# An attention and mixture-of-experts layer: expert lists built by one-hot matmuls, shared slices placed at the last experts, the last weight casts issued behind the first shared loads

## The chip, the cores and the metric

The program runs on all 8 cores of one Trainium2 chip. Each core takes 1024 of the 8192 tokens, and no core waits for another. The time of a run is the time of its slowest core in microseconds (us). Engines: PE does matmuls, DVE, ACT and POOL elementwise work and copies, POOL and SP issue most DMAs, and 16 DMA engines per core move the data.

## The reference, cut to what matters

```python
x = _layernorm(x + attn(x, Wq, Wk, Wv, Wo))          # causal, 16 heads of 128
# the feed-forward part, on flat = x (8192 tokens, 2048 wide), D_FF = 1408
h = relu(einsum('td,ndf->ntf', flat, shared_w1) + shared_b1[:, None, :])   # 2 shared experts
out = flat + einsum('ntf,nfd->td', h, shared_w2) + shared_b2.sum(0)
scores = sigmoid(flat @ centroids.T) + bias           # 16 routed experts
vals, idx = top_k(scores, 4)
gating = scatter(vals, idx); gating = gating / clip(gating.sum(-1), 1e-08)
for w1, b1, w2, b2, g in routed:                      # 16 of them
    rout += (relu(flat @ w1 + b1) @ w2 + b2) * g[:, None]
x = _layernorm(x + out + rout)
```

## The kernel before, in words

**Stages.** A core computes K and V of its sequence and attention for its 1024 rows, then the output projection `Wo` with the first norm in tiles of 128 tokens, and the gate scores. All weights come in f32. A load issued by POOL casts to bf16 on the way (`L688`, DMA `ar<-w1x`, `ar<-w2x`, one unit is 128 rows of 2048, 0.5 MB in bf16). `precast` (L237 to L244) also has POOL cast weights from DRAM to a bf16 copy in DRAM, `wpre`: 18 groups of 6 while attention runs (after 126 units there remain 36), and the rest at L545, behind the four loads of `Wo`. Units with a copy are loaded without a cast by SP (`L679`). `PRE_EXPERTS` (L43) says which experts have one: 0, 2, 4, 6, 8, 10, 12. Experts 1, 3, 5, 7, 9, 11, 13, 14, 15 are cast as they are loaded.

**The weights' ring.** Nine slots of SBUF hold units (`pump`, L691). When PE releases a slot, the next unit in order of first use is issued to it. A unit that is half used keeps its slot.

**Lists.** A token goes to four experts. A core takes per expert up to 320 rows, and a flag chooses at run time between this sparse program and one that computes all. Ranks, selection and positions are DVE operations on tiles of 128 x 128 and 128 x 2048 (L850 to L893). DVE makes destinations, then POOL writes token numbers into a DRAM list with 32 indirect scatters (L952, tensor `list_scr`) and reads it back (L961); PE transposes it (L974) and DVE makes the gather and scatter indices. Those 32 scatters run while PE does group 0 and group 1.

**Shared slices.** The two shared experts' 22 slices are cut into groups of 4, 4, 2, 2, 2, 2, 2 and 4 (`GROUPS`, L39). `dense_group` (L737) is a generator of matmul steps: `L752` is the first layer (64 steps for two slices), `L774` the second (64 steps), whose results DVE adds into the token tiles `x_tm` (`L787`). `spend(n)` takes n steps. Groups 0 and 1 are spent around the lists, groups 2 to 6 inside the experts: `FILL_AT` (L41) gives an expert's steps, in 31 portions (`tick`).

**An expert** (L1083): per slice of 128 of the hidden width, 16 matmuls `L1100` and an ACT copy; then in two halves the second layer, `L1127` and `L1133`, whose output DVE (`L1152`) and ACT (`L1154`) copy out and POOL scatters into `y_scr` (L1167). POOL gathers the next expert's rows (L1002), PE turns them (`L1017`), DVE copies them (`L1026`). From expert 13 on `combine_load` (L1056) has SP read back 1 MB blocks of `y_scr` and `combine_add` has DVE add them (`L1071`): 8 blocks per expert, the first three experts' worth inside experts 13, 14, 15, through one buffer, and 8 more in the last shared group. SP and DVE take their work in the order of the program.

## Time and profile before

| | |
|---|---|
| runs, us | 2705.9, 2714.79, 2895.99; median 2714.79 |
| the profiled execution, its own time | 2707.15 |
| span of its slowest core (core 2) | 2705.6 |
| spans of the eight cores | 2652.8 to 2705.6 |
| mean granted TensorE clock | 0.923 to 0.928 |
| busy on core 2: PE, DVE, ACT, POOL | 2249.0, 831.9, 544.7, 411.4 |
| DMA queue 0 (POOL's issues), queue 1 (SP's) | 304.39 MB, 139.90 MB |

The profiled execution lies within 0.3% of the median. Times in the trace count from the span's start: attention to 866, `Wo` and the first norm to 1094, lists and shared groups 0 and 1 to 1289, experts 0 to 15 to 2596, the last shared group and norm to the end. PE's busy time is the sum over matmuls, DMA share the mean over 16 engines; a saturated stretch reads 1.00 to 1.05.

### The profile page before, as it was taken

What the parts mean: (1) busy time and instruction counts of PE and PEld (TensorE: products, weight loads), DVE (VectorE), ACT (ScalarE), POOL (GpSimd) and SP (SyncE); (2) the same over time, 40 slices, a digit from 0 to 9 for tenths busy, and PEclk for the clock granted to TensorE, in tenths of its full rate; (3) what the DMA queues carried; (4) which work ended last, traced back from release to release, by engine and by line L of the source; (5) the groups of instructions that cost most, each with busy time, mean ns of one, the idle gap of its engine ahead of it and who ended that gap; (6) DMA issues with size and microseconds to landing.
All of it is one profiled execution on the core that took longest, in us unless ns stands there. A gap on an engine that the chain in (4) does not pass through costs nothing.

```text
span 2705.6 us, 35359 instructions; the slowest of 8 cores (2652.8 to 2705.6 us)
## 1 busy us (share of the span) xinstructions
PE 2249.0 (83%) x13390; PEld 1192.1 (44%) x13593; DVE 831.9 (31%) x1269; ACT 544.7 (20%) x817; POOL 411.4 (15%) x619
## 2 busy tenths in 40 slices
PE   5879999989888589458979999999999999576456
PEld 3546646646556244123434444454444444233121
DVE  0234434434444334143201041412213041222146
ACT  0033433334343422101111101011111111011003
POOL 1011011111110000140021212121121212111100
PEclk9889999999999689678999999999999999787788
DMA  9499999999996999912599998989898999999973
GB/s 161 65 120 121 121 122 122 121 122 120 120 118 104 160 165 139 142 46 83 170 164 264 171 242 197 205 228 176 248 180 254 175 247 196 208 222 215 202 243 125
DMA packets 114655, 446.65 MB, mean 165 GB/s; under 512 B 16244, under 2 KB 16916, under 8 KB 104752
## 3 DMA queue, kind: packets, MB, share of 16 engines
q0 software_dynamic: 81360, 304.39, 72.6%
q1 hardware_dynamic: 33120, 139.90, 15.6%
q8 instruction: 114, 1.87, 0.3%
q14 instruction: 61, 0.50, 0.1%
HBM read 647.80 MB, written 139.50 MB: 291 GB/s over the span
## 4 chain that ended last, share of the span: by engine, by line
DMA 50%; PE 36%; DVE 5%; issue 4%; another core or an unknown queue 3%; ACT 1%; POOL 1%; DVEq 0%; ACTq 0%; POOLq 0%; SPq 0%
DMA wpre<-w2x 14%; DMA wpre<-w1x 12%; DMA ar<-y_scr 10%; PE PP L1127 9%; PE PP L1100 7%; PE PP L774 5%; DMA ar<-w1x 5%; DMA ar<-w2x 5%; PE PP L1133 3%; PE PP L323 2%; PE PP L342 2%; PE PP L752 2%; DMA ar<-wqkv 2%; PE PP L1017 2%
## 5 line engine op out<-in xcount | busy, mean ns | idle before, releaser
L1100 PE MATMUL PP<-ar 128*128 128x320 bf16 x2816 | 411.4, 305 | 53.1 <-DMA ar<-w1x 48.3
L1127 PE MATMUL PP<-ar 128*128 128x512 bf16 x1363 | 373.3, 396 | 24.8 <-DMA ar<-w2x 17.4
L1100 PEld LDWEIGHTS PP<-ar 128*128 128x128 bf16 x2816 | 276.6, 100 | 188.5 <-issue 71.8
L323 PE MATMUL PP<-ar 128*128 128x512 bf16 x992 | 238.6, 383 | 30.3 <-DMA ar<-wqkv 29.1
L774 PE MATMUL PP<-ar 128*128 128x512 bf16 x680 | 191.5, 407 | 81.2 <-DVE ar L787 48.7
L478 ACT COPY ar<-PP 128x1024 bf16<-128x1024 bf16 (+1 forms) x192 | 153.4, 799 | 474.0 <-PE PP L467 474.0
L342 PE MATMUL PP<-ar 128*128 128x256 bf16 x2048 | 241.5, 273 | 0.0
L1026 DVE COPY ar<-PP 128x960 bf16<-128x960 bf16 x96 | 55.4, 598 | 587.5 <-PE PP L1017 587.5
L437 DVE TENSOR_REDUCE st_sb<-PP 128x1 f32<-128x256 f32 (+7 forms) x128 | 173.7, 1357 | 169.7 <-PE PP L431 150.5
L787 DVE SCALAR_TENSOR_TENSOR ar<-PP,ar 128x512 f32<-128x512 f32 x256 | 167.2, 687 | 167.9 <-PE PP L774 124.6
L342 PEld LDWEIGHTS PP<-ar 128*128 128x128 bf16 x2048 | 197.7, 98 | 30.3 <-issue 0.2
L1127 PEld LDWEIGHTS PP<-ar 128*128 128x128 bf16 x1408 | 121.8, 100 | 190.1 <-issue 85.0
L752 PE MATMUL PP<-ar 128*128 128x512 bf16 x669 | 162.9, 384 | 43.4 <-DMA ar<-w1x 40.1
L1107 ACT ACTIVATE ar<-PP,b_sb 128x320 bf16<-128x320 f32 x176 | 92.8, 527 | 419.3 <-PE PP L1100 404.7
L1154 ACT COPY ar<-PP 128x512 f32<-128x512 f32 x64 | 34.4, 589 | 696.0 <-PE PP L1133 696.0
L307 PE MATMUL PP<-ar 128*128 128x512 bf16 (+1 forms) x576 | 131.4, 371 | 40.2 <-DMA ar<-xT 29.5
L1071 DVE SCALAR_TENSOR_TENSOR ar<-ar,gk_sb 128x2048 f32<-128x2048 f32 x32 | 75.2, 2351 | 269.9 <-DMA ar<-y_scr 269.7
L447 ACT ACTIVATE ar<-PP,st_sb 128x256 bf16<-128x256 f32 (+7 forms) x128 | 157.0, 1226 | 0.5 <-DVE st_sb L437 0.5
L323 PEld LDWEIGHTS PP<-ar 128*128 128x128 bf16 x1024 | 97.2, 99 | 132.8 <-issue 39.2
L1133 PE MATMUL PP<-ar 128*64 128x512 bf16 x704 | 147.7, 416 | 0.3
L1167 POOL DMA_INDIRECT y_scr<-ar,sidx_sb x96 | 96.0, 1000 | 305.4 <-DVE ar L1152 284.4
L1017 PE MATMUL PP<-cb_sb,ar 128*128 128x128 bf16 (+1 forms) x768 | 97.6, 221 | 47.7 <-DVE ar L1026 45.9
(110 smaller groups left out, 1784.5 us busy)
## 6 DMA issues: line engine op xcount, KB each, us to landing
ar<-wpre SPq DMA_DIRECT2D x162, 512.0 KB
ar<-w1x POOLq DMA_DIRECT2D x117, 512.0 KB
ar<-w2x POOLq DMA_DIRECT2D x117, 512.0 KB
wpre<-w1x POOLq DMA_DIRECT2D x81, 512.0 KB, 24.7
wpre<-w2x POOLq DMA_DIRECT2D x81, 512.0 KB, 24.7
ar<-y_scr SPq DMA_DIRECT2D x32, 1024.0 KB
ar<-wqkv POOLq DMA_DIRECT2D x24, 1024.0 KB
ar<-xT POOLq DMA_DIRECT2D x8, 1024.0 KB
```

Source lines behind the costliest of these rows:

```text
L323: (lambda e, dc=dc: e.matmul(ps, w_at["k"][:, dc * 256 + jl * 128: dc * 256 + (jl + 1) * 128], x_bf[:, c * 8192 + dc * 512: c * 8192 + (dc ...
L342: (lambda e, dc=dc, tl=tl, sub=sub: e.matmul(ps[:, sub * 256:(sub + 1) * 256], x_bf[:, c * 8192 + dc * 512 + tl * 128: c * 8192 + dc * 512 ...
L437: sb.do("vector", lambda e: e.reduce_max(negmx_sp[up], PP[:, 0:kc], axis=AX.X, negate=True), "dv", 1)
L447: lambda e: e.activation(p_sb[up][:, 0:kc], PP[:, 0:kc], AF.Exp, bias=negmx_sp[up], scale=1.0, accum_out=lsum_sp[up]),
L478: lambda e: e.copy(dst, tb[:, 0:nbl * 128].rearrange("p (kb n) -> p kb n", n=128)), "ac", 1)
L752: m = sb.mm((lambda e, dc=dc, w=w, bank=bank, nt=nt: e.matmul(psum_bank(bank), w[:, dc * 128:(dc + 1) * 128], xhat[:, dc * 1024 + nt * 512 ...
L774: m = sb.mm((lambda e, j=j, w=w, bank=bank, ti=ti, dn=dn, last=last: e.matmul(psum_bank(bank), Hs[j][:, ti * 128:(ti + 1) * 128], w[:, dn ...
L787: give_bank(bank, sb.vec((lambda e, xs=xs, bank=bank, sc=sc: e.scalar_tensor_tensor(xs, psum_bank(bank), sc, xs, ALU.mult, ALU.add))))
L1017: m = sb.mm((lambda e, n=n, dc=dc, t=t, rows=rows: e.transpose(tb[:, n * CAP + t * 128: n * CAP + t * 128 + rows], xg[t][0:rows, dc * 128: ...
L1100: m = sb.mm((lambda e, dc=dc, w=w, bank=bank: e.matmul(psum_bank(bank)[:, 0:CAP], w[:, dc * 128:(dc + 1) * 128], xgT[:, dc * CAP:(dc + 1) ...
L1127: sb.mm((lambda e, fc=fc, w=w, po=po, t=t, dn=dn: e.matmul(psum_bank(2 * t + dn), Hr(fc)[:, t * 128:(t + 1) * 128], w[:, po * 1024 + dn * ...
L1133: m = sb.mm((lambda e, fc=fc, w=w, po=po, dn=dn, end=end: e.matmul(PP[dn * 64:(dn + 1) * 64, 4 * 512:5 * 512], Hr(fc)[:, 256:CAP], w[:, po ...
```

## The change

It has five parts.

1. The lists. Each (expert, token tile) pair gets one DVE operation that compares the row of slot numbers with the token's position, 128 x 320 in bf16, and one matmul of that one-hot block against two columns per expert (token number within the tile; eight times the choice plus the tile's number plus one). 128 such pairs accumulate in one PSUM bank over twelve buffers. The result is copied, transposed and decoded into the same indices. The DRAM list, its fill, 32 scatters, 4 loads and the destination arithmetic go.
2. The stored gates and their transposes move behind that loop; 96 steps of group 0 stand inside it, 6 per expert.
3. `FILL_AT`: 64 at experts 3, 7, 11 and 12 and 128 at 13, 14 and 15, where it was 128 at 3, 5, 7, 9 and 11.
4. `PRE_EXPERTS`: 14 in the place of 12.
5. Behind `Wo` only 16 casts are issued; the last 20 come behind the first eight shared loads. The sparse program stands ahead of the dense one.

DVE also waits for the last write of a piece of `x_tm` before it adds to it again (`x_mark`).

```diff
-FILL_AT = {0: 72, 3: 128, 5: 128, 7: 128, 9: 128, 11: 128}
+FILL_AT = {0: 72, 3: 64, 7: 64, 11: 64, 12: 64, 13: 128, 14: 128, 15: 128}
-PRE_EXPERTS = (0, 2, 4, 6, 8, 10, 12)
+PRE_EXPERTS = (0, 2, 4, 6, 8, 10, 14)
...
-        precast(len(PRE_UNITS))
+        precast(PRE_WO)
...
         set_plan(plans["common"] if plans else [])
+        precast(len(PRE_UNITS))
         state["gen"] = dense_group(GROUPS[0], nt_outer=True)
...
+        sb.vchain(lambda e: e.tensor_scalar(pos, sel, -FAR, FAR - SHIFT, ALU.mult, ALU.add))
+        pos_dv = sb.vchain(lambda e: e.tensor_tensor(pos, pos, pbank[:, 0:128], ALU.add))
+        sb.vchain(lambda e: e.memset(vz, 0.0))
...
+        sb.wait("tensor", *vz_dv)
+        sb.wait("tensor", *pos_dv)
+        sb.wait_all("vector", u_stored)
+        for n in range(16 * 8):
+            ei, ti = divmod(n, 8)
+            buf = n % len(one_hot)
+            if oh_free[buf] is not None:
+                sb.wait("vector", *oh_free[buf])
+            m = sb.vec(lambda e, buf=buf, c=ti * 16 + ei: e.tensor_scalar(
+                one_hot[buf], iota_sb, pos[:, c:c + 1], None, ALU.is_equal))
+            if ti == 0:
+                spend(6)
+            sb.wait("tensor", *m)
+            oh_free[buf] = sb.mm((lambda e, buf=buf, n=n, c=ti * 512 + ei * 32: e.matmul(
+                pbank[0:32, 0:CAP], vz[:, c:c + 32], one_hot[buf],
+                start=(n == 0), stop=(n == 127), skip_group_check=True)), True)
...
-        for c in range(8 * KR):
-            sb.dma("gpsimd", (lambda e, c=c: e.indirect_dma_start(
-                out=list_scr, out_offset=IOA(ap=dest_sb[:, c:c + 1], axis=0),
...
-            if b % 2:
-                spend(6)
+            spend(3)
...
-            if j == 12:
+            if j == NR - 1:
                 spend(100000)
...
+                with e.If(flag < 1):
+                    play(e, sparse_ops[eng])
                 with e.If(flag > 0):
                     play(e, dense_ops[eng])
-                with e.If(flag < 1):
-                    play(e, sparse_ops[eng])
```

POOL's issues from the loads of `Wo` on. Before (`L242` is a cast into `wpre`, `L688` a casting load into the ring):

```order
L242 DMA wpre<-w1x 128x2048 x3
L242 DMA wpre<-w2x 128x2048 x11
L242 DMA wpre<-w1x 128x2048 x11
L242 DMA wpre<-w2x 128x2048 x11
L688 DMA ar<-w1x 128x2048 x4
L688 DMA ar<-w2x 128x2048 x4
```

and now (one line down or up: `L246` is the cast, `L687` the load, `L1028` the gather of expert 0):

```order
L246 DMA wpre<-w1x 128x2048 x3
L246 DMA wpre<-w2x 128x2048 x11
L246 DMA wpre<-w1x 128x2048 x2
L687 DMA ar<-w1x 128x2048 x4
L687 DMA ar<-w2x 128x2048 x4
L246 DMA wpre<-w1x 128x2048 x9
L246 DMA wpre<-w2x 128x2048 x11
L1254 TENSOR_LOAD flag_sb
L1255 COMPARE_AND_BRANCH
L1028 DMA ar<-u_scr,gidx_sb 128x2048 x2
L1028 DMA ar<-u_scr,gidx_sb 64x2048
```

The eight shared loads now stand behind 16 casts instead of 36, and the other 20 casts stand ahead of the flag and the gathers.

DVE in the list stage. Before, behind the last of the destination arithmetic:

```order
L890 TENSOR_REDUCE ar<-ar 128x8
L891 SCALAR_TENSOR_TENSOR ar<-ar 128x128
L892 TENSOR_REDUCE gk_sb<-ar 128x8
L893 CAST dest_sb<-ar 128x32
L787 SCALAR_TENSOR_TENSOR ar<-PP,ar 128x512 x5
L903 MEMSET ar 18x1024
L905 CAST ar<-PP 16x512
L906 CAST ar<-PP 16x512
L787 SCALAR_TENSOR_TENSOR ar<-PP,ar 128x512 x27
```

and now (`L903` is the one-hot comparison, `L789` the addition into `x_tm` that was `L787`); the pattern of the last rows goes on over 16 experts:

```order
L883 TENSOR_TENSOR ar<-ar,PP 128x128
L886 MEMSET ar 128x4096
L889 CAST ar<-cf_sb 128x8x16
L890 SCALAR_TENSOR_TENSOR ar<-ar,cf_sb 128x8x16
L903 TENSOR_SCALAR ar<-cb_sb,ar 128x320
L789 SCALAR_TENSOR_TENSOR ar<-PP,ar 128x512
L903 TENSOR_SCALAR ar<-cb_sb,ar 128x320 x8
L789 SCALAR_TENSOR_TENSOR ar<-PP,ar 128x512
L903 TENSOR_SCALAR ar<-cb_sb,ar 128x320 x8
L789 SCALAR_TENSOR_TENSOR ar<-PP,ar 128x512 x2
L903 TENSOR_SCALAR ar<-cb_sb,ar 128x320 x8
```

Each eight comparisons are followed by one or two additions that wait for PE.

PE at expert 5. Before, its first layer (`L1100`) with shared steps (`L752`) between:

```order
L1127 MATMUL PP<-ar 128x512 x4
L1133 MATMUL PP<-ar 64x512 x2
L1100 MATMUL PP<-ar 128x320 x16
L752 MATMUL PP<-ar 128x512 x4
L1100 MATMUL PP<-ar 128x320 x16
L752 MATMUL PP<-ar 128x512 x4
L1100 MATMUL PP<-ar 128x320 x16
L752 MATMUL PP<-ar 128x512 x4
```

and now, with `L1127` as the first layer, `L1154`, `L1160` as the second, `L1146` as the reset of a bank:

```order
L1154 MATMUL PP<-ar 128x512 x4
L1160 MATMUL PP<-ar 64x512 x2
L1154 MATMUL PP<-ar 128x512 x4
L1160 MATMUL PP<-ar 64x512 x2
L1127 MATMUL PP<-ar 128x320 x176
L1146 MATMUL PP<-ar,cb_sb 128x512
L1154 MATMUL PP<-ar 128x512 x4
L1160 MATMUL PP<-ar 64x512 x2
L1154 MATMUL PP<-ar 128x512 x4
```

The shared steps are gone from expert 5; rows such as those of before now stand at experts 12 to 15, where before there was one row of 176.

## Rows read from the trace of the kernel before

**Rows 1.** Page of the slowest core: mean busy tenths of its 16 DMA engines, 40 slices.
```profile
DMA  9499999999996999912599998989898999999973
```

**Rows 2.** Windows: span; PE, PEld, DVE, ACT, POOL busy (count); PEclk, DMA share, GB/s.
```profile
1579.00:1655.00 76.00, 74.61 (x435) 36.69 (x438) 23.68 (x38) 9.03 (x17) 13.69 (x15) 0.98 0.89 251
...
1655.00:1730.00 75.00, 72.20 (x402) 35.33 (x408) 11.16 (x18) 9.43 (x17) 18.45 (x29) 1.00 1.01 176
...
1760.00:1765.00 5.00, 5.00 (x39) 3.62 (x37) 0.00 (x0) 1.05 (x2) 2.36 (x3) 1.00 0.99 319
...
2187.00:2273.00 86.00, 85.26 (x492) 40.70 (x497) 23.91 (x39) 9.07 (x18) 19.52 (x23) 1.00 0.88 239
```

**Rows 3.** Timeline around the first shared weights: start, duration (us), engine, line [idle before].
```profile
996.04 0.52 POOL L242 DMA_DIRECT2D wpre<-w1x  x1 [7.12 <-DMA wpre<-w2x]
...
1111.98 0.52 POOL L242 DMA_DIRECT2D wpre<-w2x  x1 [5.83 <-DMA wpre<-w2x]
...
1112.54 2.15 POOL L688 DMA_DIRECT2D ar<-w1x  x4
...
1134.23 11.39 PE L752 MATMUL PP<-ar 128*128 128x512 bf16 x38 [40.15 <-DMA ar<-w1x]
```

**Rows 4.** Timeline of the list stage, DVE, POOL and PE.
```profile
1162.89 0.23 DVE L857 CAST ar<-ar 128x128 bf16<-128x128 f32 x1
...
1164.99 2.29 DVE L879 TENSOR_TENSOR ar<-ar,cb_sb 128x2048 bf16<-128x2048 f32 x1
...
1181.35 0.91 DVE L903 MEMSET ar<- 18x1024 bf16 x1 [0.34 <-DVE ar L787]
...
1218.35 0.97 POOL L952 DMA_INDIRECT list_scr<-cf_sb,dest_sb  x1 [0.30 <-issue]
...
1238.92 27.57 PE L752 MATMUL PP<-ar 128*128 128x512 bf16 x124 [1.77 <-issue]
```

**Rows 5.** DVE groups by form: count, busy us, mean ns of one, idle before.
```profile
L453 DVE TENSOR_SCALAR ar<-ar,st_sb 128x512 bf16<-128x512 bf16 x16 | 5.6, 353 | 1.7
...
L453 DVE TENSOR_SCALAR ar<-ar,st_sb 128x256 bf16<-128x256 bf16 x16 | 4.6, 286 | 1.7
...
L787 DVE SCALAR_TENSOR_TENSOR ar<-PP,ar 128x512 f32<-128x512 f32 x256 | 167.2, 687 | 167.9 <-PE PP L774 124.6
```

**Rows 6.** Timeline in attention: a POOL issue beside a DVE operation.
```profile
374.59 0.88 POOL L242 DMA_DIRECT2D wpre<-w2x  x1 [4.62 <-DMA wpre<-w2x]
...
374.73 0.62 DVE L453 TENSOR_SCALAR ar<-ar,st_sb 128x1536 bf16<-128x1536 bf16 x1
```

**Rows 7.** Timeline, ACT and DVE copies that close experts 0, 1, 2, 4, 11, 12, 15.
```profile
1368.65 1.07 ACT L1154 COPY ar<-PP 128x512 f32<-128x512 f32 x2 [25.93 <-PE PP L1133]
...
1451.51 1.07 ACT L1154 COPY ar<-PP 128x512 f32<-128x512 f32 x2 [20.68 <-PE PP L1133]
...
1516.88 1.07 ACT L1154 COPY ar<-PP 128x512 f32<-128x512 f32 x2 [21.41 <-PE PP L1133]
...
1667.95 1.07 ACT L1154 COPY ar<-PP 128x512 f32<-128x512 f32 x2 [19.52 <-PE PP L1133]
...
2213.96 1.07 ACT L1154 COPY ar<-PP 128x512 f32<-128x512 f32 x2 [25.75 <-PE PP L1133]
...
2272.95 1.07 ACT L1154 COPY ar<-PP 128x512 f32<-128x512 f32 x2 [17.12 <-PE PP L1133]
...
2595.59 1.88 DVE L1152 COPY ar<-PP 128x512 f32<-128x512 f32 x3
```

**Rows 8.** Timeline, first casting loads of experts 1 and 3, and one in a saturated stretch.
```profile
1489.78 0.58 POOL L688 DMA_DIRECT2D ar<-w1x  x1 [32.50 <-PE PP L1133]
...
1860.35 0.53 POOL L688 DMA_DIRECT2D ar<-w2x  x1 [2.86 <-DMA ar<-w2x]
```

**Rows 9.** Timeline, one DVE add of a combined row block in expert 13.
```profile
2319.01 2.35 DVE L1071 SCALAR_TENSOR_TENSOR ar<-ar,gk_sb 128x2048 f32<-128x2048 f32 x1 [11.58 <-DMA ar<-y_scr]
```

More of the change, by code:

```diff
@@ L231, in build_nc @@
     g_sb = carve(77056, 256, F32)
+    lrow = carve(77312, 2 * LCAP, F32)
+    vz = carve(23552, 4096)
+    one_hot = [carve(98304 + CAP * i, CAP) for i in range(12)]
     def emit(plans):
@@ L252, in emit @@
         ]
-        sb.vec(lambda e: e.memset(fill_sb[:, :], EMPTY))
-        sb.wait("sync", "dv")
-        fill_mark = sb.dma("sync", lambda e: e.dma_start(out=list_scr.rearrange("(p j) c -> p (j c)", p=128),
-                                                         in_=fill_sb[:, :]))
         def load_w(kind, g):
@@ L732, in emit @@
         hs_free = [None]
+        x_mark = {}
         def w2_kind(ge):
@@ L786, in dense_group @@
                     xs = x_tm[ti][:, dn * 512:(dn + 1) * 512]
-                    give_bank(bank, sb.vec((lambda e, xs=xs, bank=bank, sc=sc: e.scalar_tensor_tensor(
-                        xs, psum_bank(bank), sc, xs, ALU.mult, ALU.add))))
+                    if (ti, dn) in x_mark:
+                        sb.wait("vector", *x_mark[ti, dn])
+                    x_mark[ti, dn] = sb.vec((lambda e, xs=xs, bank=bank, sc=sc: e.scalar_tensor_tensor(
+                        xs, psum_bank(bank), sc, xs, ALU.mult, ALU.add)))
+                    give_bank(bank, x_mark[ti, dn])
                 if after_tile is not None:
@@ L915, in emit @@
         saved = ({k: (dict(v) if k in ("at", "load") else v and list(v)) for k, v in ring.items()},
-                 {b: list(v) for b, v in rb.items()}, list(hs_free))
+                 {b: list(v) for b, v in rb.items()}, list(hs_free), dict(x_mark))
         sb = root.branch_off()
@@ L936, in emit @@
         sb = root.branch_off()
-        ring, rb, hs_free = saved
+        ring, rb, hs_free, x_mark = saved
         saved = None
@@ L947, in limit @@
             return limit_regs[value]
-        sb.wait("gpsimd", *dest_dv)
-        sb.wait("gpsimd", *fill_mark)
-        for c in range(8 * KR):
-            sb.dma("gpsimd", (lambda e, c=c: e.indirect_dma_start(
-                out=list_scr, out_offset=IOA(ap=dest_sb[:, c:c + 1], axis=0),
-                in_=rid_sb[:, c:c + 1], in_offset=None,
-                bounds_check=limit(e, NR * LCAP - 1), oob_is_err=False)), pool="gs")
-        sb.wait_all("gpsimd", sb.dma_total_marks("gs"))
-        list_rows = list_scr.rearrange("(e s) c -> e (s c)", e=16)
-        lrow = tmp[9]
-        list_marks = []
-        for r0, s0, n, c0 in ((0, 0, 128, 0), (16, 128, 128, 0), (32, 256, 64, 0), (32, 256, 64, 64)):
-            list_marks.append(sb.dma("gpsimd", (lambda e, r0=r0, s0=s0, n=n, c0=c0: e.dma_start(
-                out=lrow[r0:r0 + 16, c0:c0 + n], in_=list_rows[:, s0:s0 + n])), pool="gs"))
         def chain_groups():
@@ L1072, in combine_add @@
             ybufs.append([buf, m, None])
+            for dn in range(4):
+                x_mark[ti, dn] = m
         pend = []
```

101 lines of the change are left out of this document (57 added, 44 removed).

## The prediction

> **What bounds the kernel now.** I read the page's slices first. DMA is at nine tenths or more in most slices from attention to the end, with two holes: the list stage (2 in slice 18) and the very end [rows 1]. So from expert 1 on one has to ask of every change both what it does to PE and what it does to DMA. Second, two windows that follow each other and make up one period of the pattern of a plain and a casting expert: in the second, PE is busy 72 of 75 us and DMA reads 1.01, in the first PE is busy 74.6 of 76 us and DMA 0.89, the clock nearly full in both [rows 2]. The middle is bound by PE and DMA almost equally. Third, the timeline where the first shared weights arrive: PE starts its first shared matmul at 1134.2 after 40.15 us idle, so it was done with `Wo` and the gate scores at 1094.1. It waited for a load that POOL issued only at 1112.5, after its last cast [rows 3]. Fourth, the ends of experts: 0 ends at 1368.7, 1 at 1451.5, 2 at 1516.9, 4 at 1668.0, 11 at 2214.0, 12 at 2273.0, 15 at 2595.6 [rows 7]. Three facts are in these. Experts 3 and 4, with 128 shared steps, took 151.1 us; experts 1 and 2, with none, took 148.2; experts 13, 14, 15 took 322.6, or 107.5 each, with no shared steps at all but 8 blocks of `y_scr` each.
>
> **Prices of transfers.** Two casting loads in a saturated stretch stand 3.4 us apart (0.53 and the 2.86 before it), and several such in a row average 3.3; I take 3.28 [rows 8]. A plain unit is 0.52 MB at the 319 GB/s of a stretch that has only such loads, 1.64 us [rows 2]. An expert's scatter and gather are some 3.4 MB at that rate, 11 us (an estimate). A pair then needs 26 x 3.28 + 22 x 1.64 + 22 = 143 us; the two windows give 76 x 0.89 + 75 x 1.01 = 143 as well. In experts 13 to 15, (107.5 - 72 - 11) / 8 leaves 3.1 us for each block. The chain of reads alone costs the same: 11.58 us of waiting and 2.35 of adding, 13.9 x 8 = 111 [rows 9]. So there both DMA and the one buffer bind.
>
> **Part 5, the casts behind the first loads.** The 16th cast behind `Wo` went out at 996.0 and the last, the 36th, at 1112.0: 5.8 us each [rows 3]. Now POOL is through with 16 at 996, and the loads wait only for their slots, the first of which the last `Wo` tile frees some ten us before 1094 (three of its four sets of 16 matmuls at 0.22 us come after). The DMA queue is then empty of casts, and units land every 3.3 us while PE takes 16 x 0.216 = 3.5 us for each half of a slice. PE goes on at 1094: 40 us saved. After the wait PE ran 38 matmuls in 11.39 us, 0.300 each, where 124 full-speed ones took 27.57 with their gaps, 0.22 [rows 3, 4]: 3 us more. Together -43. The other 20 casts go behind 8 loads (27 us from 1083): 1110 + 16 x 5.8 = 1203 for the last issue. They stand ahead of the flag and of expert 0's gather, which is due at about 1235 (below). They fit into the hole of the list stage, with 32 us to spare; without that cover each us is paid in full at expert 0.
>
> **Parts 1 and 2, the lists.** Before, from the selection (`L857`, 1163.1) to group 1 (`L752`, 1238.9) passed 75.8 us, though the 32 scatters ended only at 1219.3 [rows 4]. PE was never held by the list itself, so its removal frees nothing directly; what goes is PE's slow crawl beside the scatters. New: two operations of 2.3 us (`L879` and its sum, moved up), seven small ones (2 us), and a memset of 4096 columns, four times the 0.91 us for 1024 [rows 4]: 10 us, with PE idle. Then the loop. A comparison is a `TENSOR_SCALAR` in bf16 from SBUF: 286 ns at 256 columns, 353 at 512, hence 303 at 320 [rows 5]. Per expert: 8 x 0.303 = 2.4, one and a half additions at 0.687 = 1.0, and about 0.6 in which DVE waits for the four shared matmuls ahead of the addition. That is 4.0, and 64 us for sixteen. PE's 8 small matmuls run behind the comparisons. Bounds: below, 128 x 0.303 and half the additions hidden, 47; above, every comparison at the 0.687 of `L787`, 88. Then thirteen small operations (5.5), the last 32 shared steps with their additions (5.5), the gate transposes (2). In all 87 against 75.8: +11, with bounds of -6 and +35. Five more small DVE operations ahead of the gather cost +2. The additional DVE waits (`x_mark`) are for work of a whole group earlier and cost nothing, since the same 32 additions stand between.
>
> The Trainium skill (VectorE: DVE Perf Modes, "The perf-mode tier table") says that a scalar operation on bf16 in SBUF runs at four elements per cycle. The slope of rows 5, 67 ns for 256 columns, agrees; what it does not shrink is the fixed 0.22 us, which is three quarters of each comparison.
>
> **Parts 3 and 4, experts.** Fill is 64 less at experts 3, 7, 11 and 128 less at 5, 9. A casting expert is not bound by PE once its fill is gone. A pair with 64 steps loads 24 casts, 137 us; with none, 130. I keep the idle 8 us per pair (76 x 0.11, where slots are full and the next casts not yet due [rows 2]): 145 and 138 against 151. Four pairs: -(6 + 13) x 2 = -38. Bounds: experts 1 and 2 show 148 without fill, which would give -10; PE alone (128 x 0.216 = 27.6 us) would give -83. Experts 11 to 15 get what the others lose: 12 casts, 39 us. Expert 12 took 59 us because its loads were plain; with 24 casts it needs about 90. Expert 14, now plain, gives the same back. Against that, the idle DMA time in expert 12 (86 x 0.12 = 10 us [rows 2]) goes, and about 9 more (an estimate) where casts waited for slots behind the block reads. Tail: +39 - 19 = +20. The fill's PE work, 27.6 us an expert, finds room in 107.5 us, since experts without it are done by PE in 59 (expert 12). Its additions, 32 x 0.69, lie on DVE between block adds, in the 11.6 us in which DVE waits anyway. Experts together: -18.
>
> The sum: -43 + 11 + 2 - 18 = -48. From the execution's own 2707.15 that is 2659; the median of the runs is 0.3% above it, and I say 2660.
>
> **Rivals.**
>
> *DMA overlaps better* (0.24). The idle 8 us per pair disappear too, since PE now waits for slots less, and the list loop comes near its lower bound. For: the clock and both engines have no other limit there. Against: experts 1 and 2. 2707 - 43 - 6 + 2 - 55 = 2605.
>
> *Moved, not saved* (0.12). The experts are one long DMA queue and gain nothing: 2707 - 43 + 13 = 2677. For it speak experts 1 and 2, against it that their casts began only 15 us before the expert, where expert 3's began 27 us before [rows 7, 8].
>
> *POOL is held up by the comparisons* (0.08). A cast's issue that lay beside one comparison-like operation took 0.88 us instead of 0.52 [rows 6]. If POOL can't issue while DVE goes through 128 of them, the 16 late casts slip by up to 64 us, to 1267, the gather lands 20 us behind that instead of at about 1242, and expert 0 starts 45 us late: 2704. One row with 0.36 us more speaks rather for a cost of a few us in the slack. The Trainium skill (SBUF — State Buffer, "A bandwidth-pool intuition that's wrong (but worth ruling out)") describes that: POOL can't write descriptors until the vector operation releases a port that they share.
>
> *The tail pays in full* (0.14), the one that ends slower. In experts 13 to 15 DVE waits in program order for a block read; PE's fill needs DVE for every four steps and has three banks. If PE can't get ahead, fill and waiting add instead of overlapping: 3 x 27.6 = 83, and 34 at expert 12, tail +117. With -30 from the front and -39 in the middle that is 2755. It decides from a tail of +69 on. For: PE's work is small in 107.5 us there, and yet nothing goes faster. Against: DVE is idle in each wait, the additions stand ahead of the block add in its order, and four steps of an expert with fill fill the 13.9 us.
>
> **How the numbers follow.** Forecast 0.42, own range 2635 to 2685. A measurement of this kernel tells about 2% from no change: 2660. The forecast lies on that line, so I split it 0.20 and 0.22. Faster by over 2%: 0.20 + 0.24 = 0.44. Within: 0.22 + 0.12 + 0.08 and 0.06 of the tail's rival, 0.48. Slower: 0.08. The range goes from just below the better overlap, 2598, to 2715, which leaves out the tail's rival.
>
> **What would show it.** PE's wait of 40 us before the first shared step gone; the last cast issued at about 1203 and ahead of the first gather; comparisons near 0.30 us, the loop near 64; group 1 starting 32 us earlier than now, expert 0 about 30; experts 5 and 6 in 138, 12 in about 90, 13 to 15 in 310 to 330 together. I am wrong if experts 3 to 10 give under 20 or over 60 us, if 13 to 15 take over 360, or if POOL's issues stretch beside the comparisons.

## The result, and the profile after

The changed kernel ran in 2636.41, 2642.31 and 2644.44 us, median 2642.31, against 2714.79 before: a ratio of 0.9744, with a 95% interval of 0.9692 to 0.9797. (Executions in which the cores of one die ran at a lower granted clock are left out of every comparison; the experiment with the comparisons ahead has only two others, and in its profile, where cores 4 to 7 had 0.80 to 0.81, a core of the other die is read.) The profiled execution took 2636.41 us where that of before took 2707.15, so 70.7 less; the forecast had 48 less. Below, the numbers of before stand in the rows ahead of the prediction.

The page of the slowest core (again core 2, span 2634.7 us), granted clock and DMA share in 40 slices:

```profile
PEclk9989999999999779999999999999999998999888
DMA  9499999999998895597499898989898999989973
```

Against [rows 1] the list stage is no longer empty (slices 17 and 18, counted from 0, read 9 and 7 instead of 1 and 2), but slices 15 and 16 ahead of it now read 5 and 5: a new hole.

Timeline where the first shared weights arrive, as in [rows 3]: start, duration, engine, line (`L598` is `Wo`, `L687` a casting load, `L246` a cast into `wpre`, `L1028` the gather):

```profile
1081.21 2.14 POOL L687 DMA_DIRECT2D ar<-w1x  x4 [81.68 <-PE PP L598]
...
1092.09 8.58 PE L752 MATMUL PP<-ar 128*128 128x512 bf16 x39
...
1200.81 0.52 POOL L246 DMA_DIRECT2D wpre<-w2x  x1 [4.15 <-DMA wpre<-w2x]
...
1236.72 1.07 POOL L1028 DMA_INDIRECT ar<-u_scr,gidx_sb  x1 [35.39 <-DVE ar L789]
```

PE goes from the gate scores to the first shared step without a wait. The last cast is issued at 1200.8 (forecast 1203), 36 us ahead of the gather, which is issued at 1236.7 (forecast 1235).

The list stage, as in [rows 4, 5]. First the end of the selection and the loop on DVE and PE (`L861` closes the selection as `L857` did before, `L903` is the comparison, `L908` its matmul, `L789` the addition into `x_tm`), then the group of all 128 comparisons (busy us, mean ns), then the start of group 1:

```profile
1117.94 0.23 DVE L861 CAST ar<-ar 128x128 bf16<-128x128 f32 x1
...
1125.21 3.47 DVE L886 MEMSET ar<- 128x4096 bf16 x1 [0.99 <-DVE ar L883]
...
1147.99 1.78 DVE L903 TENSOR_SCALAR ar<-cb_sb,ar 128x320 bf16<-128x320 bf16 x8
...
1149.94 1.47 PE L774 MATMUL PP<-ar 128*128 128x512 bf16 x6
1150.87 0.69 DVE L789 SCALAR_TENSOR_TENSOR ar<-PP,ar 128x512 f32<-128x512 f32 x1 [1.09 <-PE PP L774]
...
1151.91 1.57 PE L908 MATMUL PP<-ar 128*32 128x320 bf16 x7 [0.27 <-DVE ar L903]
```

```profile
L903 DVE TENSOR_SCALAR ar<-cb_sb,ar 128x320 bf16<-128x320 bf16 x128 | 28.6, 296 | 0.0
```

```profile
1204.90 27.57 PE L752 MATMUL PP<-ar 128*128 128x512 bf16 x127
```

DVE waits 1.09 us for PE's six shared steps, then PE waits 0.27 for DVE's next comparison: the two take turns. The loop runs from 1129.9 to 1190.0.

The copies of ACT that close experts 0, 2, 10, 11 and 12, as in [rows 7] (now `L1181`), and PE's first step of the last shared group:

```profile
1336.31 1.07 ACT L1181 COPY ar<-PP 128x512 f32<-128x512 f32 x2 [24.27 <-PE PP L1160]
...
1480.62 1.07 ACT L1181 COPY ar<-PP 128x512 f32<-128x512 f32 x2 [20.91 <-PE PP L1160]
...
2030.76 1.07 ACT L1181 COPY ar<-PP 128x512 f32<-128x512 f32 x2 [19.52 <-PE PP L1160]
...
2109.45 1.07 ACT L1181 COPY ar<-PP 128x512 f32<-128x512 f32 x2 [0.89 <-PE PP L1160]
...
2196.31 1.07 ACT L1181 COPY ar<-PP 128x512 f32<-128x512 f32 x2 [23.84 <-PE PP L1160]
...
2516.49 27.80 PE L752 MATMUL PP<-ar 128*128 128x512 bf16 x128
```

In the kernel before, expert 10 ended at 2125.3 and PE took the last shared group up at 2579.0, some 17 us before DVE's copy at 2595.6 that [rows 7] have as the end of expert 15:

```profile
2125.32 1.07 ACT L1154 COPY ar<-PP 128x512 f32<-128x512 f32 x2 [20.71 <-PE PP L1133]
...
2578.95 27.80 PE L752 MATMUL PP<-ar 128*128 128x512 bf16 x125
```

Windows, columns as in [rows 2]: the new hole, a pair without shared steps (experts 5 and 6), and expert 13, 14, 15:

```profile
1003.00:1040.00 37.00, 34.14 (x217) 17.58 (x216) 16.84 (x34) 10.19 (x7) 0.00 (x0) 0.95 0.56 138
1040.00:1081.00 41.00, 41.00 (x258) 20.23 (x256) 21.12 (x46) 9.26 (x8) 0.00 (x0) 1.00 0.07 26
...
1620.00:1696.00 76.00, 63.37 (x364) 30.94 (x363) 7.68 (x14) 8.34 (x16) 17.21 (x25) 0.96 1.02 205
1696.00:1755.00 59.00, 59.00 (x360) 29.84 (x359) 7.13 (x13) 7.94 (x15) 12.90 (x16) 1.00 0.86 237
...
2197.00:2311.00 114.00, 92.64 (x483) 42.44 (x482) 42.71 (x51) 10.88 (x20) 19.88 (x28) 0.91 1.00 231
2311.00:2405.00 94.00, 87.58 (x486) 41.84 (x483) 45.18 (x52) 10.41 (x19) 12.57 (x18) 1.00 0.89 252
2405.00:2518.00 113.00, 88.90 (x444) 39.88 (x445) 42.84 (x48) 10.60 (x20) 19.98 (x32) 0.92 1.00 214
```

In the pair without shared steps the casting expert has PE busy 63 of 76 us with DMA full, so only DMA binds there; in the plain expert behind it PE is busy all 59 us and DMA 0.86. In experts 13 and 15 DMA is full and PE has 21 and 24 us to spare; in expert 14, whose loads are plain, DMA reads 0.89 and PE has 6.

Where the 70.9 us between the spans went, stage by stage, each from the rows above and those of before:

| stage | before | after | change | forecast |
|---|---|---|---|---|
| start to the end of the selection | 1163.1 | 1118.2 | -45.0 | -43 |
| selection to group 1 | 75.8 | 86.7 | +10.9 | +11 |
| group 1 to the end of expert 0 | 129.7 | 131.4 | +1.7 | +2 |
| experts 1 and 2 | 148.2 | 144.3 | -3.9 | 0 |
| experts 3 to 10 | 608.4 | 550.1 | -58.3 | -38 |
| expert 11 to PE's last group | 453.6 | 485.7 | +32.1 | +20 |
| from there to the end | 126.7 | 118.2 | -8.5 | 0 |

The column of before is core 2, and for the list stage that matters. From the end of the selection to group 1 the other cores of its die (0 to 3) took 75 to 81 us in the same profile, but cores 4 to 7 only 47 to 50. In the changed kernel all eight take 86 to 88. In the kernel before, while the 32 scatters run, DVE on cores 0 to 3 stands idle for 3 to 11 us before single additions, with no releaser in the profile; on core 2 the four matmuls that an addition needs had ended 2 to 7 us before it began. PE goes on when the addition is done. Core 2 of the kernel before, then core 5, where the same steps run without a break:

```profile
1202.04 0.69 DVE L787 SCALAR_TENSOR_TENSOR ar<-PP,ar 128x512 f32<-128x512 f32 x1 [5.65 <-remote]
1202.88 1.86 PE L774 MATMUL PP<-ar 128*128 128x512 bf16 x4 [5.32 <-issue]
...
1210.48 0.69 DVE L787 SCALAR_TENSOR_TENSOR ar<-PP,ar 128x512 f32<-128x512 f32 x1 [7.75 <-issue]
...
1220.26 0.69 DVE L787 SCALAR_TENSOR_TENSOR ar<-PP,ar 128x512 f32<-128x512 f32 x1 [9.10 <-remote]
```

```profile
1185.03 23.10 PE L774 MATMUL PP<-ar 128*128 128x512 bf16 x105
```

Four such gaps of DVE on core 2 come to 26 us; cores 4 to 7 have none above 2 us. So the slowest core of cores 4 to 7 went only from 2675.6 to 2631.2, 44 us, where the slowest of all went from 2705.6 to 2634.7. In each of the 21 runs of the kernel before that list their cores, the slowest core of one die, always the same die of a chip, was 11 to 39 us above that of the other; in the six of the changed kernel the two lay within 9 us. Only one of the 21 was profiled. That the others lose the time in the same way is likely but not shown, and why one die has the gaps is open.

### The profile page after: what moved, and what is told of

Its sections match the earlier page's. It is cut to its first block, busy times and chain, and to the rows that moved or that the text cites. A ratio compares the mean times of both kernels' runs of the same rounds, so it can differ in the third digit from the quotient of the medians.

```text
span 2634.7 us, 36044 instructions; the slowest of 8 cores (2594.9 to 2634.7 us)
## 1 busy us (share of the span) xinstructions
PE 2296.7 (87%) x13723; PEld 1200.7 (46%) x13723; DVE 865.8 (33%) x1397; ACT 544.2 (21%) x817; POOL 377.8 (14%) x583
## 4 chain that ended last, share of the span: by engine, by line
DMA 49%; PE 38%; DVE 6%; issue 4%; ACT 2%; POOL 1%; DVEq 0%; POOLq 0%; SPq 0%; ACTq 0%
DMA wpre<-w1x 12%; DMA wpre<-w2x 12%; DMA ar<-w2x 8%; PE PP L1154 8%; PE PP L1127 8%; DMA ar<-y_scr 6%; DMA ar<-w1x 5%; PE PP L774 4%; PE PP L598 3%; PE PP L1160 3%; PE PP L752 2%; PE PP L1043 2%; PE PP L322 2%; PE PP L341 2%; DVE ar L1096 1%
## 5 line engine op out<-in xcount | busy, mean ns | idle before, releaser
L1127 PE MATMUL PP<-ar 128*128 128x320 bf16 x2816 | 413.0, 305 | 44.0 <-DMA ar<-w1x 37.4
L1154 PE MATMUL PP<-ar 128*128 128x512 bf16 x1408 | 379.6, 394 | 17.5 <-DMA ar<-w2x 17.4
L1127 PEld LDWEIGHTS PP<-ar 128*128 128x128 bf16 x2816 | 276.4, 99 | 182.6 <-issue 64.2
L322 PE MATMUL PP<-ar 128*128 128x512 bf16 x1024 | 244.4, 382 | 29.4 <-DMA ar<-wqkv 29.3
L774 PE MATMUL PP<-ar 128*128 128x512 bf16 x704 | 208.4, 411 | 68.2 <-DVE ar L789 47.5
L789 DVE SCALAR_TENSOR_TENSOR ar<-PP,ar 128x512 f32<-128x512 f32 x256 | 169.8, 688 | 218.8 <-PE PP L774 203.3
L1154 PEld LDWEIGHTS PP<-ar 128*128 128x128 bf16 x1408 | 124.7, 100 | 189.4 <-issue 76.9
L752 PE MATMUL PP<-ar 128*128 128x512 bf16 x704 | 174.0, 382 | 12.8 <-DVE ar L890 8.8
L1181 ACT COPY ar<-PP 128x512 f32<-128x512 f32 x64 | 34.4, 589 | 633.5 <-PE PP L1160 633.5
L1160 PE MATMUL PP<-ar 128*64 128x512 bf16 x704 | 146.8, 414 | 0.0
L466 PE MATMUL PP<-cb_sb,ar 128*128 128x128 bf16 x1152 | 101.3, 227 | 37.5 <-ACT ar L477 32.5
L687 POOL DMA_DIRECT2D ar<-w1x x117 | 65.1, 561 | 450.7 <-PE PP L1160 247.2
```

Of the source, the lines that this page charges most:

```text
L322: (lambda e, dc=dc: e.matmul(ps, w_at["k"][:, dc * 256 + jl * 128: dc * 256 + (jl + 1) * 128], x_bf[:, c * 8192 + dc * 512: c * 8192 + (dc ...
L752: m = sb.mm((lambda e, dc=dc, w=w, bank=bank, nt=nt: e.matmul(psum_bank(bank), w[:, dc * 128:(dc + 1) * 128], xhat[:, dc * 1024 + nt * 512 ...
L774: m = sb.mm((lambda e, j=j, w=w, bank=bank, ti=ti, dn=dn, last=last: e.matmul(psum_bank(bank), Hs[j][:, ti * 128:(ti + 1) * 128], w[:, dn ...
L789: x_mark[ti, dn] = sb.vec((lambda e, xs=xs, bank=bank, sc=sc: e.scalar_tensor_tensor(xs, psum_bank(bank), sc, xs, ALU.mult, ALU.add)))
L1127: m = sb.mm((lambda e, dc=dc, w=w, bank=bank: e.matmul(psum_bank(bank)[:, 0:CAP], w[:, dc * 128:(dc + 1) * 128], xgT[:, dc * CAP:(dc + 1) ...
L1154: sb.mm((lambda e, fc=fc, w=w, po=po, t=t, dn=dn: e.matmul(psum_bank(2 * t + dn), Hr(fc)[:, t * 128:(t + 1) * 128], w[:, po * 1024 + dn * ...
```

## Experiments

Twelve kernels on three chips, four on each; ratios are to the kernel before on the same chip, with 95% intervals. The kernel before had medians of 2705.2, 2704.2 and 2735.2 on the three. The changed kernel ran in the first comparison (0.9744, chip not noted) and on the second of the three chips. The table below gives, from each profile, what groups of experts took (start of DVE's copy that closes one to the next, to 0.2 us, slowest core unless a core is named), and the time from the end of expert 12 to the end of the program:

| kernel | expert 0 ends | 1, 2 | 3 to 10 | 11, 12 | 13 to 15 | 12 to the end |
|---|---|---|---|---|---|---|
| before (first profile) | 1368.7 | 148.3 | 608.4 | 147.6 | 322.6 | 432.6 |
| changed (first profile) | 1336.3 | 144.4 | 550.1 | 165.5 | 321.9 | 438.3 |
| changed again, core 0 / core 4 | 1335.2 / 1330.5 | 142.4 / 141.9 | 548.2 / 550.0 | 165.7 / 164.3 | 337.2 / 327.9 | 449.4 / 443.6 |
| all casts at `Wo` | 1379.8 | 147.7 | 547.3 | 165.3 | 327.0 | 442.4 |
| only part 5 | 1379.9 | 148.8 | 599.0 | 148.8 | 321.8 | 429.3 |
| old `FILL_AT` and `PRE_EXPERTS` | 1334.5 | 141.9 | 599.5 | 147.6 | 326.5 | 441.9 |
| old `FILL_AT` alone | 1329.4 | 141.3 | 603.7 | 155.0 | 317.4 | 433.0 |
| lists alone | 1393.0 | 150.9 | 607.8 | 147.1 | 324.8 | 433.6 |
| more steps in the tail, core 0 / core 4 | 1324.2 / 1346.8 | 141.8 / 143.9 | 522.6 / 540.9 | 157.1 / 167.0 | 356.3 / 353.3 | 476.0 / 470.4 |
| sixteen more casts | 1383.8 | 144.6 | 551.1 | 155.5 | 322.2 | 439.3 |
| twelve casts in the hole | 1351.0 | 147.0 | 555.8 | 154.3 | 319.4 | 435.7 |
| hole and ahead | 1347.2 | 148.3 | 553.8 | 157.0 | 321.2 | 435.2 |
| the same, even fill | 1346.7 | 147.7 | 569.1 | 154.7 | 323.0 | 441.3 |

Two things in the cores bear on every reading. In each of the neighbouring pairs of cores (0 and 1, 2 and 3, 4 and 5, 6 and 7) one is slower, in the changed kernel by 21 to 41 us, and which of the two it is differs from execution to execution. In the first profile of the changed kernel the slower four (0, 2, 4, 7) took 550 to 555 us for experts 3 to 10, the faster four 525 to 536. The slower four set the time, so only slower cores are compared with slower ones. The other is the difference between the dies of the kernel before: where it matters, runs are set against its faster die too.

### Which part carries the gain

**Part 5 undone.**

```diff
-PRE_WO = 16
+PRE_WO = 162
```

> The changed kernel with all 36 casts behind Wo again (part 5 undone). My theory: PE again waits some 40 us for the first shared weights, nothing later absorbs it, because expert 0 has idle DMA time either way: 40 to 44 us slower than the changed kernel, group 1 starting some 41 us later than at 1205, experts 1 to 15 as they are. Rival (one long DMA queue: the casts cost the same wherever they stand, so an earlier start of the experts is given back there): 0 to 15 us slower.

Measured: ratio 0.9912 (0.9877 to 0.9947), runs from 2681.57 to 2685.68 us; by the ratios 37 to 45 us above the changed kernel. The wait is back:

```profile
1138.91 10.68 PE L752 MATMUL PP<-ar 128*128 128x512 bf16 x39 [39.12 <-DMA ar<-w1x]
```

Expert 0 ends 43.5 us later, experts 3 to 10 take 547.3. Nothing absorbs it, and the rival of one long queue falls.

**Part 5 alone.**

```diff
-        precast(len(PRE_UNITS))
+        precast(16)
...
+        precast(len(PRE_UNITS))
         state["gen"] = dense_group(GROUPS[0], nt_outer=True)
```

> The kernel before with part 5 alone: 16 casts behind Wo, 20 behind the first eight shared loads, lists by 32 indirect scatters as before. My theory: part 5 needs part 1. PE starts the shared steps at 1094 instead of 1134, but the scatters stand behind the last cast on POOL (about 1203), end at about 1244 and the gather is issued at about 1258 instead of 1269; PE runs out of shared steps and waits. About 11 us faster than before, at most 20. Rival (the parts are independent): 40 us faster than before.

Measured: 1.002 (0.9996 to 1.0043), nothing won; I had expected 11 us. The two dies are within 13 us of each other now: on the die that was faster before (slowest core 2673 to 2683 us) the kernel is some 32 us slower (2703 to 2722), on the other it is level. Timeline of PE and POOL (`L242` a cast, `L953` a scatter into the list, `L975` the list's transpose):

```profile
1094.37 8.58 PE L752 MATMUL PP<-ar 128*128 128x512 bf16 x39
...
1277.68 0.31 PE L975 MATMUL PP<-cf_sb,ar 48*128 48x48 f32 x1 [77.86 <-DMA ar<-list_scr]
```

```profile
1214.24 0.52 POOL L242 DMA_DIRECT2D wpre<-w2x  x1 [6.52 <-DMA wpre<-w2x]
1228.53 1.06 POOL L953 DMA_INDIRECT list_scr<-cf_sb,dest_sb  x1 [13.77 <-issue]
...
1267.91 0.97 POOL L953 DMA_INDIRECT list_scr<-cf_sb,dest_sb  x1 [0.27 <-issue]
```

PE starts 40 us earlier and then waits 78 us for the list. The mechanism was the one expected, its size was not: the casts went out at 6 us each until 1214, and another 13.8 us passed before the first scatter, put down to no releaser (8 to 14 us on the eight cores). Expert 0 ends 11 us later than in the first profile of before.

**Parts 1 and 2 alone.** The diff is that of the first experiment together with both old tables.

> The changed kernel with parts 3, 4 and 5 undone: the new lists alone, all casts behind Wo, the old FILL_AT and PRE_EXPERTS. My theory: alone they cost what their stage shows, +10.9 us in the list stage and some 2 ahead of the gather, and save nothing; 8 to 14 us slower than before, the DMA engines idle for some 60 us in the list stage. Rival (they shorten something by themselves, the POOL engine free of 32 scatters): not slower than before.

Measured: one run, 2734.47, against runs of before from 2727.98 to 2741.96 on that chip. No interval: on the slowest core it shows no large gain or loss, and neither the 8 to 14 us nor the rival is settled by it. From the first shared step to group 1 pass 115.0 us in its profile against 104.7 on core 2 of before, so the stage's own loss of 10 is there; cores 4 to 7 of before took 75 to 78. The runs show more: on the chip's faster die the slowest core had 2702 to 2704 us before and has 2722.9 now, 20 us more, on the slower die 2726 to 2740 and 2732.4. With the gaps away the new lists alone cost time.

Read together, by the slowest core: lists alone about nothing, casts alone nothing, both together (the next kernel) 0.9841. On the faster die: 20 us lost, 32 lost, and 13 won (2676 to 2662 us on the first chip). The parts are complements: the lists free POOL, and that gives the late casts a place. But of the 40 us that they give together some 27 are the difference of the dies, which either part alone also removes.

**Parts 3 and 4 undone.**

```diff
-FILL_AT = {0: 72, 3: 64, 7: 64, 11: 64, 12: 64, 13: 128, 14: 128, 15: 128}
-PRE_EXPERTS = (0, 2, 4, 6, 8, 10, 14)
+FILL_AT = {0: 72, 3: 128, 5: 128, 7: 128, 9: 128, 11: 128}
+PRE_EXPERTS = (0, 2, 4, 6, 8, 10, 12)
```

> The changed kernel with the old FILL_AT and the old PRE_EXPERTS (parts 3 and 4 undone). My theory: the stretch from expert 3 to the end is what these two parts decide; it took 1188.7 us before and 1154.1 after, so 35 us slower than the changed kernel (30 to 40), experts 3 to 10 near 608 and experts 13 to 15 near 322. Rival (part of the middle's gain beyond the forecast comes from the new front, through the state in which the ring enters expert 1): 10 to 20 us slower, experts 3 to 10 near 590.

Measured: 0.9841 (0.9810 to 0.9871). The changed kernel has 0.9775 on the second chip and 0.9744 in the first comparison, so 18 to 26 us, less than the 35 expected and near the rival's 10 to 20; but the rival's 590 for the middle did not come. Experts 3 to 10 took 599.5, not 608; the kernel with part 5 alone, whose middle is that of before, took 599.0 too, and in the first profile of before the seven other cores took 596 to 601. So some 8 us of the first comparison's 58 belong to core 2 of that execution and not to the edit. The tail spreads between cores of one execution: for experts 13 to 15, by ACT's copies, the four slower cores of the changed kernel took 318 to 322 us in the first profile and 314 to 335 in the second.

From expert 12 to the end this kernel needs 433 to 442 us on its slower cores and lists alone 434 to 439, against 428 to 434 in before and in part 5 alone, which have the same tables. So some 5 us come with the new program itself. The added waits (`x_mark`) would be a reason; they were not tried alone.

**`FILL_AT` alone undone.**

> The changed kernel with the old FILL_AT alone; expert 12 is still cast as it loads and 14 is plain. My theory: shared steps cost 1 us for 8 in the casting experts of the middle and almost nothing in experts 13 to 15, where DMA and the block reads bind: experts 3 to 11 take 68 us more, 12 some 3 to 6 less, 13 to 15 within 10 us of 321, the end 7 less: 50 us slower (40 to 60). Rival (the shared steps of the tail are paid there too): experts 13 to 15 get up to 83 us faster, and the kernel stays within 10 us of the changed one.

Measured: 0.9833 (0.9803 to 0.9862), level with the kernel before it, so 16 to 24 us above the changed one. Both theories miss: experts 3 to 11 take 62 more where 68 were expected, experts 13 to 15 get only 4.5 faster (10 to 20 against the second chip), not 83; what I had wrong is expert 12, at 67.4 instead of 84, though it casts. A reason, which no run here separates, is that behind a 128-step expert 11, in which PE sets the pace, DMA gets ahead by what nine slots hold. The two experts together take 155.0 against 165.5.

**Still more in the tail.**

```diff
-FILL_AT = {0: 72, 3: 64, 7: 64, 11: 64, 12: 64, 13: 128, 14: 128, 15: 128}
+FILL_AT = {0: 72, 11: 64, 12: 64, 13: 192, 14: 128, 15: 192}
```

> The changed kernel with the 64 shared steps of experts 3 and 7 moved on to 13 and 15 (192 each). My theory: 64 steps in a pair of the middle cost 4 to 10 us (138.7 and 144.2 against 133.6 without), and in experts 13 and 15 PE still has 20 us to spare, so 10 to 15 us faster. Rival (the tail is full: the clock is already 0.91 to 1.00 there and PE is busy 93 of 114 us in expert 13): experts 13 and 15 get up to 14 us longer each and the kernel is 5 to 15 us slower.

Beside it ran the changed kernel once more:

> The changed kernel once more, on the chip on which the next three run, so that they have it beside them. The first profile gave 2636.41 us; 2634 to 2645 is expected, experts 3 to 10 together 550 us within 5, the stretch from expert 13 to 15 within 5 of 322.

Measured: changed again 0.9775 (0.9747 to 0.9803), more steps 0.9831 (0.9777 to 0.9885), runs of 2649 to 2671 against 2643 to 2646. The intervals overlap, but every run is slower, by 22 us in the median: the rival has the direction, and it costs more than its 5 to 15. Core 0 is the faster of its pair in the one profile and the slower in the other, so it can't be compared. Over the four slower cores of each, experts 3 to 10 give back 8 us (552 to 543 in the mean) and 13 to 15, by ACT's copies, take 26 more (325 to 351). The changed kernel once more came as expected in the middle, but 13 to 15 took 337.2 in it, outside its band.

From these runs the price of 64 shared steps follows. In experts 3 to 10: 550.1 with two such portions, 599 to 604 with eight, hence 8 to 9 us each; but the first two cost only about 4 each (the 8 us above). In the tail the first six portions cost 15 to 30 us together (experts 11 to 15: 472.4 without, 487.4 to 502.9 with), 2.5 to 5 each, and the next two about 14 each (490 to 518 for experts 11 to 15 over the slower cores). The table of the changed kernel lies about where the two prices meet.

### What sets the list loop

```diff
+        LEAD = 6
-        for n in range(16 * 8):
+        for step in range(16 * 8 + LEAD):
...
-            sb.wait("tensor", *m)
+            sb.wait("tensor", *oh_done[n])
```

The comparison of step n is issued by DVE before the shared steps and the matmul of step n - 6.

> The changed kernel with the one-hot comparisons running six ahead of their matmuls. My theory: the list loop (60 us, 3.70 an expert) is bound neither by DVE's comparisons (8 x 0.222 = 1.78 an expert) nor by PE, but by the two taking turns: DVE waits 1.09 or 0.83 us per expert for the four shared matmuls, PE 0.3 to 0.7 for the next comparison. With the turns gone DVE binds at 1.78 + 1.03 = 2.8 an expert, 45 us: 12 to 15 us faster, all of it seen at expert 0. Rival (PE's own work, 6 shared steps and 8 small matmuls, is the limit): within 4 us of the changed kernel.

Measured: 0.9715 (0.9686 to 0.9743) against 0.9775 (0.9747 to 0.9803) on the same chip; 2626.84 and 2629.46 us against a median of 2642.85, so 15 us. It is faster than both kernels, if by two runs only. Core 3, DVE (`L906` is the comparison here) and then PE:

```profile
1138.69 1.78 DVE L906 TENSOR_SCALAR ar<-cb_sb,ar 128x320 bf16<-128x320 bf16 x8
1140.39 1.32 DVE L789 SCALAR_TENSOR_TENSOR ar<-PP,ar 128x512 f32<-128x512 f32 x2
1141.62 1.78 DVE L906 TENSOR_SCALAR ar<-cb_sb,ar 128x320 bf16<-128x320 bf16 x8
```

```profile
1185.59 27.57 PE L752 MATMUL PP<-ar 128*128 128x512 bf16 x127
```

From the third expert on no wait is left on DVE; two experts take 5.23 us instead of 7.39, and the comparisons run from 1126.3 to 1170.4. Expert 0 ends at 1321.2 on both slower cores of the die, 9 and 14 us earlier than on those of the changed kernel on that chip, and the gain is still there at the end.

### Where more casts fit

**Sixteen more, in the list stage and expert 0.**

```diff
+    units += [... the first 16 units of expert 12 ...]
...
-        precast(len(PRE_UNITS))
+        precast(len(PRE_UNITS) - len(pre_mark) - EXTRA + EXTRA_EARLY)
...
+                if j == 0 and step % 2 == 0:
+                    precast(1)
```

> The changed kernel with 16 units of expert 12 cast ahead of time as well, 6 of them behind the last casts in the list stage and 10 inside expert 0, where the DMA engines are 0.47 to 0.58 busy. My theory: DMA time that stands idle before expert 1 is worth as much as any; 16 casts are 52 us of it against 51 idle, and expert 12 then loads 16 units plain, 26 us less: 15 to 25 us faster, expert 12 at 62 to 70 instead of 87. Rival (POOL in its order: ten casts at 4.8 us hold up the scatters of expert 0 and the first casting loads of expert 1): expert 1 ends 20 us later and nothing is left of it.

Measured: 0.9879 (0.9857 to 0.9902), 31 us slower than the changed kernel beside it. Neither mechanism: it is not POOL's order that holds the kernel up, but PE's waits for landings. Expert 0 ends some 50 us late; experts 1 and 2 take 144.6, as before. PE waits for the gathered rows and, in expert 0, for plain loads:

```profile
1264.01 0.26 PE L1046 MATMUL PP<-cb_sb,ar 128*128 128x128 bf16 x1 [15.50 <-DMA ar<-u_scr,gidx_sb]
...
1302.94 3.31 PE L1132 MATMUL PP<-ar 128*128 128x320 bf16 x16 [3.18 <-DMA ar<-wpre]
```

DMA issues of the stretch 1260 to 1330 (KB each, median us from issue to landing):

```profile
ar<-wpre SPq DMA_DIRECT2D x11, 512.0 KB, 24.4
wpre<-w1x POOLq DMA_DIRECT2D x5, 512.0 KB, 24.9
```

A plain load that needs 1.64 us of DMA time lands 24 us after its issue beside four casts, and the ring has only nine slots. The Trainium skill (DMA: Bandwidth & Descriptors, "Queues, rings and completion order") says that a DMA engine serves the queues that have work in turn, packet by packet; the two kinds of transfer with equal landing times fit that. The added casts did not spread over the idle time either: DMA reads 1.00 from 1243 to 1264, while the gather lands, 0.12 from there to 1283, and 0.99 from 1283 to 1330, where PE is busy 33 of 47 us. A DMA share of 0.58 in a stretch that PE drains in step is not 0.42 of free time.

**Twelve, into the hole.** 28 casts behind `Wo`, and 12 units of expert 12 more.

```diff
-PRE_WO = 16
+PRE_WO = 28
+    units += [("w1", 14, u) for u in range(FCH)] + [("w2", 14, 0)]
```

> The changed kernel with 28 casts behind Wo instead of 16, and 12 units of expert 12 cast ahead of time as well; 20 casts remain behind the first shared loads. My theory: the change opened a hole of its own, DMA 0.56 busy from 1003 to 1040 and 0.07 from there to 1081, as the ring's loads must wait for slots; 12 casts at 5.8 us fill it without touching anything, and expert 12 loads 12 units plain: 12 x 1.64 = 20 us less DMA in a stretch bound by it, 12 to 20 us faster (expert 12 at 70 to 76). Rival (as with the sixteen casts, the time comes back as waits: the casts collide with the norm's stores and the first loads): PE restarts later than 1092 and at most 5 us are won.

Measured: 0.9708 (0.9668 to 0.9749). The changed kernel did not run on this chip; against its 0.9775 and 0.9744 that is 10 to 18 us, with intervals that overlap, and the kernel before is 30 us slower on this chip than on the others. On the faster die of before it is 54 us below it, the changed kernel on the second chip 42, which gives 12. Windows of the same stretches:

```profile
1003.00:1040.00 37.00, 30.42 (x190) 15.06 (x192) 16.95 (x34) 8.57 (x7) 2.06 (x4) 0.98 0.99 184
1040.00:1081.00 41.00, 40.27 (x245) 20.53 (x250) 18.34 (x36) 10.92 (x8) 4.12 (x8) 0.94 1.00 132
```

The hole is full, no wait has come at the first shared step, and experts 11 and 12 take 154.3 instead of 165. But the casts are not free: from the first matmul of `Wo` to the last of the gate scores the slower cores take 129 to 130 us with 28 casts there, 120 to 127 in the kernels with 16, and 127 to 130 in those with all 36. That expert 0 ends at 1351.0 is mostly the chip, on which the kernel with the lists alone had 1393.0 and that with all casts at `Wo` 1379.8 on the first. The gain is where it was expected, less some 6 us in the `Wo` stage; its size in the runs is only probable.

**Both together, and an even fill.** The table of the last one is `{0: 72, 3: 64, 5: 64, 7: 64, 9: 64, 11: 64, 12: 64, 13: 64, 14: 128, 15: 64}`.

> The twelve casts in the hole together with the comparisons six ahead. My theory: the two gains lie in different stages and add: 28 to 36 us faster than the changed kernel, about 2610. Rival (the faster list loop brings the gather in among the last casts, which now end at the same 1200 while the gather comes at 1217): the second gain is cut to under 8, about 2620.

> The same with FILL_AT of 64 at experts 3, 5, 7, 9, 11, 12, 13 and 15 and 128 at 14. My theory: in a casting expert of the middle DMA binds, so 64 steps cost there only their own two to four casts and little PE time, 2 to 10 us, while 64 steps in 13 or 15 cost 5 to 6 us, so it is within 8 us of the run before it, either way. Rival (every shared step in the middle is paid with its 0.216 us, as the 54 us between 64 at two experts and 128 at four suggest): 15 to 20 us slower than the run before it.

Measured: 0.9737 (0.9690 to 0.9784) and 0.9728 (0.9668 to 0.9787), no better than the twelve casts alone (0.9708). The gains do not add: expert 0 ends only 4 us earlier than with the twelve casts, and the rival named the reason. The last cast now goes out at 1220.7 with the gather at 1233.4, and PE waits for its rows:

```profile
1251.23 0.27 PE L1052 MATMUL PP<-cb_sb,ar 128*128 128x128 bf16 x1 [11.56 <-DMA ar<-u_scr,gidx_sb]
```

In the changed kernel the same wait is 1.48. The even fill is level in the runs (medians 2658.6 and 2658.5) and its profile shows the shift: 15 us more in experts 3 to 10, over the slower cores 8 of them in experts 5 and 6 and 11 in 9 and 10, and nothing gained in 13 to 15. Runs and profiles differ here because the profile of the first of the two is its fastest run (2643.1 of 2643 to 2666) and that of the second its slowest (2660.7), so the comparison of the fills is open.

## Why the prediction was right, and where it was off

The time came within 1% of the forecast, but the profile gave 71 us where 48 were forecast, and experts 3 to 10, the tail and the end were off, in both directions.

**Part 5** was right to 2 us, and the rows bear each step: no wait at 1092, the last cast at 1201, 36 us of slack before the gather. One thing was not seen: the last of the 16 casts is issued at 999, the ring cannot load before 1081, and DMA runs nearly dry between. The prediction noted an empty queue at 1083 as a benefit and did not ask what it cost.

**The lists** came to 86.7 against 87, and that is in part luck. The prelude was 11.8 against 10, the memset 3.47 against 3.6. A comparison lasts 296 ns, as forecast (303), but the next one starts 212 ns after it, so 128 cost 28 us and not 39. The waits were larger in turn: 0.83 and 1.09 us per expert instead of 0.6. The run with the comparisons ahead shows that the turns, not the comparisons, set the loop. What the prediction missed is the other side of the difference. It put the 75.8 us of core 2 down to "PE's slow crawl beside the scatters" and did not look at another core: on cores 4 to 7 the same scatters ran beside the same steps in 47 to 50 us, so that there the new lists cost 37 to 39 us and not 11. The forecast holds for the die that set the time.

**Experts 3 to 10** are the term that was mis-sized: -38 forecast, -58 in the profiles, about -50 against the other baselines (599 with part 5 alone, 596 to 601 on the other cores of the first profile). The failed step is "a pair with 64 steps 145, with none 138": measured were 138.7 and 144.2, and 134.4 and 132.8. I priced 64 steps by their two casts alone, 6.6 us. They cost 8 to 9 for the six that left, and about 4 for the last two. A reading that fits both, but that no run separates, is that with 128 steps PE was as near its limit as DMA (72 of 75 us in [rows 2]), so that taking them away relieves both.

**The tail** was +32 to PE's last group against +20, and the end behind it -8.5 against 0, so +24 together: near the forecast, but not by its terms. Expert 12 took 86.9 (forecast 90). The prediction took DVE's copy at 2595.6 for the end of expert 15 and got 322.6 us for experts 13 to 15; by that copy they are within a microsecond of before. PE was through at 2579.0, so it took 306.0 us for them before (the 3.1 us worked out for each block would be 2.4 by that) and takes 320.2 now: the shared steps cost it 14 us there. DVE no longer lags behind PE at the end, which fits the shorter end, though no run separates the two. Its detail "with 24 casts it needs about 90" holds only if DMA has not got ahead; behind a full expert 11 it was 67.4.

**The rivals.** *DMA overlaps better* had about the size of the middle, but not its mechanism: in the plain expert of the pair without shared steps DMA still reads 0.86, 8 us idle, and the list loop did not come near its lower bound. *Moved, not saved* fell with the middle. *POOL held up*: casts beside the comparisons took 0.52 to 0.57 us to issue, and their pace was 4.8 us, faster than before. The lock itself is in [rows 6]: the issue ends at 375.47, 0.12 us after the DVE operation at 375.35. The Trainium skill (SBUF — State Buffer, "A bandwidth-pool intuition that's wrong (but worth ruling out)") gives 115 ns from the end of such an operation, and the row agrees. Beside the comparisons, of 0.3 us each, at most 0.05 us of it are seen. *The tail pays in full* fell: 384 steps less brought 5 to 20 us there, not 83. The wrong-if bound of 60 us for experts 3 to 10 was just not reached.

## What to carry to other kernels

Work that is moved into a hole needs two things free, the resource and the queue that issues it: here neither new lists nor moved casts were worth anything alone, and together they gave 40 us on the slowest core and 13 on the faster die. Before filling a stretch with transfers, look at who waits for a landing in it; a stretch with 0.07 of DMA and no reader took twelve casts for some 6 us, one with 0.58 and a reader every 2.8 us charged nearly their full time. When two engines take turns in a loop, let the producer run a few steps ahead before making either faster. Before pricing a stage from the slowest core, read the same stage on the others; a term that only one die has is no property of the work.
